# A graph layer with linear attention and experts: rows of x turned beside the products that use them, and attention outputs computed the other way round in two parts

## What is computed

```python
xn = layernorm(x)
# graph part: normalised neighbour sums of h
h = xn @ gnn_W.T + gnn_b
out_g[row] += deg[row]**-0.5 * deg[col]**-0.5 * h[col]      # over all edges and self loops
# linear attention, 16 heads of 64, 256 random features
q, k, v = (xn @ W.T + b for W, b in ...)                      # split into heads
phi(y) = (exp(y @ orf.T / 64**0.25 - |y|**2 / 16) + 1e-6) / 16
kv = phi(k).T @ v ; ksum = phi(k).sum(0)                       # [256, 64], [256] per head
att = (phi(q) @ kv) / (phi(q) @ ksum)                          # per head, rows are nodes
x = x + out_g + att @ Wo.T + bo
# experts: best 2 of 8 by a gate, on layernorm(x)
x = x + ffn(layernorm(x))
```

## Time and profile before

| | |
|---|---|
| median of 3 runs | 1444.85 us (1444.17 to 1446.24) |
| the profiled execution | 1449.3 us, span 1447.7 us |
| TensorE clock granted, mean | 0.97 |
| PE busy | 1359.6 us (94%) |
| DVE busy | 790.5 us (55%) |
| ACT busy | 563.6 us (39%) |
| POOL busy | 395.8 us (27%) |

### The profile page before, as it was taken

One profiled execution on the slowest core, in us unless ns is written; L12 is line 12 of the kernel. 1 busy time (PEld: TensorE's weight loads), 2 busy tenths in 40 slices (PEclk: granted clock), 3 DMA queues, 4 the chain that ended last, 5 costly groups with the idle time before them and its releaser, 6 DMA issues.

```text
span 1447.7 us, 25316 instructions
## 1 busy us (share of the span) xinstructions
PE 1359.6 (94%) x8199; PEld 1201.9 (83%) x8234; DVE 790.5 (55%) x1648; ACT 563.6 (39%) x943; POOL 395.8 (27%) x407
## 2 busy tenths in 40 slices
PE   5899999999989999999999999998999599999996
PEld 2476677899989999999999999987888588888885
DVE  7866444446355656565656565655454634444641
ACT  7322232211044544545454555553222224444541
POOL 7532543244330001010101010003223133333432
PEclk9899999999998999999999999999999599999998
DMA  4111211264410000000000000003245467777853
GB/s 167 49 30 37 66 48 59 77 193 147 119 35 14 30 14 20 24 18 26 16 27 14 29 14 29 0 30 112 57 153 174 172 190 222 219 214 212 275 143 56
DMA packets 58101, 127.78 MB, mean 88 GB/s; under 512 B 7626, under 2 KB 28826, under 8 KB 58048
## 3 DMA queue, kind: packets, MB, share of 16 engines
q1 hardware_dynamic: 48016, 96.79, 20.3%
q0 software_dynamic: 10032, 30.30, 8.6%
HBM read 91.46 MB, written 37.43 MB: 89 GB/s over the span
## 4 chain that ended last, share of the span: by engine, by line
PE 81%; DVE 8%; issue 4%; ACT 3%; DMA 2%; POOL 1%; DVEq 1%; POOLq 0%; SPq 0%; ACTq 0%
PE PB L1757 7%; PE PB L1759 7%; PE PB L1758 7%; PE PB L1663 7%; PE PB L1973 6%; PE PB L1974 6%; PE PB L1976 6%; PE PB L1795 5%; PE PB L1818 4%; PE PB L1742 3%; PE PB L1743 2%; PE PB L1702 2%; PE PB L1744 2%; PE PB L1703 2%; PE PB L1704 2%
## 5 line engine op out<-in xcount | busy, mean ns | idle before, releaser
L1757 PE MATMUL PB<-xh,hw 128*128 128x416 f32 (+1 forms) x576 | 205.6, 357 | 0.0
L1759 PE MATMUL PB<-xh,hw 128*128 128x416 f32 (+1 forms) x576 | 204.5, 355 | 0.0
L1758 PE MATMUL PB<-xl,hw 128*128 128x416 f32 (+1 forms) x576 | 204.4, 355 | 0.0
L1973 PE MATMUL PB<-mwh,mth 128*128 128x512 f32 x368 | 148.5, 404 | 0.6 <-issue 0.6
L1974 PE MATMUL PB<-mwl,mth 128*128 128x512 f32 x368 | 144.2, 392 | 0.0
L724 POOL CAST hw<-hraw 128x1024 fp32r<-128x1024 f32 x24 | 25.0, 1040 | 429.2 <-DVE qphi L1333 207.1
L1663 PE MATMUL PB<-ohs,ohd 128*128 128x512 bf16 (+1 forms) x530 | 114.4, 359 | 16.7 <-DVE ohs L1209 14.4
L1663 PEld LDWEIGHTS PB<-ohs,ohd 128*128 128x128 bf16 x564 | 49.2, 101 | 80.4 <-DVE ohs L1209 43.9
L1209 DVE TENSOR_SCALAR ohs<-iota,sc 128x1280 bf16<-128x1280 f16 x188 | 113.9, 606 | 0.0
L1976 PE MATMUL PB<-mwh,mtl 128*128 128x512 f32 x368 | 113.9, 391 | 0.0
L1757 PEld LDWEIGHTS PB<-xh,hw 128*128 128x128 f32 x576 | 109.9, 191 | 1.4
(11 more groups left out here) (303 smaller groups left out, 3080.4 us busy)
## 6 DMA issues: line engine op xcount, KB each, us to landing
mraw<-expert_w SPq DMA_DIRECT2D x64, 512.0 KB, 9.1
count_rests<-ATf POOLq DMA_DIRECT2D x9, 640.0 KB, 3.5
xrow<-x SPq DMA_DIRECT2D x40, 128.0 KB, 2.9
y_scratch<-xrow SPq DMA_DIRECT2D x40, 128.0 KB, 2.1
yrow<-y_scratch SPq DMA_DIRECT2D x20, 256.0 KB, 3.0
x2n_half<-xhat SPq DMA_DIRECT2D x20, 256.0 KB, 2.3
out<-x SPq DMA_DIRECT2D x9, 512.0 KB
ATf<-wg SPq DMA_DIRECT2D x32, 128.0 KB, 2.3
```

Source lines behind the costliest of these rows:

```text
L1757: mm(bank(i, n), hw[:, wi, 0, k, :], xh[:, k, c0:c0 + n], start=(k == 0), stop=False)
L1758: mm(bank(i, n), hw[:, wi, 0, k, :], xl[:, k, c0:c0 + n], start=False, stop=False)
L1759: ins = mm(bank(i, n), hw[:, wi, 1, k, :], xh[:, k, c0:c0 + n], start=False, stop=(k == KT - 1))
L1973: mm(y[c], mth[:, k, :], mwh[par][:, k, c * CW:(c + 1) * CW], start=(k == 0), stop=False)
```

## The change

Two edits in different stages.

*Head.* (a) Row tile t+1 is turned on TensorE just before product tile t, instead of all ten ahead of the first; tile 0 is turned before block 0. Turned tiles share the PSUM banks of the block that is not being built (TURN_BLOCK). (b) The normalisation of a row tile goes from GpSimd to ScalarE (scale and shift in one pass), for seven tiles at the start and for the last three before block 1. (c) The lows of a quarter of the weights go from GpSimd to VectorE, behind the one-hots of blocks 0, 1, 3 and 6. The raw ring has eight slabs. ScalarE rounds a quarter ahead of a block. (d) `rest_squares(b-1)` comes before the end of block b. (e) The two conversions of the edge lists stand later in VectorE's first chain, and block 0 needs one register load less.

*Attention.* (f) The output product is turned round: stationary is the key-value matrix, moving are the query features over a third of the nodes, and the result has features on partitions, as attnT wants it. The transposes and their copies go. (g) Both operands are split in rounded part and rest: ScalarE adds epsilon and rounds in a second pass after each exponential (qh), VectorE makes the rest (ql) in place of its epsilon pass. (h) The key-value matrix has 128 columns: 64 values and 64 copies of the sum of keys, in one buffer for both heads, so head 1's is made only after outputs(0, 2). (i) VectorE takes reciprocals over 64 partitions x 417 elements and multiplies into attnT. There are three outputs per head, laid between the projections in a new order.

```diff
+TURN_BLOCK = (0, 0, 0, 0, 1, 1, 1, 1, 2, 2)
+EARLY = 7
...
+        def turn_bank(i):
+            return bank(3 * ((TURN_BLOCK[i // 2] + 1) % 2) + i % 3)
...
@@ sync: raw slabs
-                if i >= 4:
-                    sp.wait_ge(w_ready, i - 3)
+                if i >= KT:
+                    sp.wait_ge(w_ready, i - KT + 1)
...
@@ gpsimd
-                g.tensor_scalar(xn_tile(t), xn_tile(t), negmean[:, t:t + 1], rstd[:, t:t + 1], ALU.add,
-                                ALU.mult).then_inc(s_xn, 1)
+                g.tensor_tensor(shift[:, t:t + 1], negmean[:, t:t + 1], rstd[:, t:t + 1], ALU.mult).then_inc(s_shift, 1)
...
+            for t in range(EARLY):
+                row_scale(t)
             degrees(0)
+            for t in range(EARLY, TT):
+                row_scale(t)
+            for b in range(1, TT):
                 degrees(b)
...
@@ scalar
+            def normalize(t):
+                act.wait_ge(s_shift, t + 1)
+                a.activation(xn_tile(t), xn_tile(t), ACT.Identity, bias=shift[:, t:t + 1],
+                             scale=rstd[:, t:t + 1]).then_inc(s_xn, 1)
...
+            normalize_rows(0, EARLY)
             high_quarter(0)
             for i in range(TILES):
                 q, t = i // TT, i % TT
                 if i in BREAKS:
-                    keep_block(BREAKS.index(i) + 1)
-                if i in (11, 22):
-                    high_quarter(2 + i // 22)
+                    b = BREAKS.index(i) + 1
+                    if b in (1, 3, 6):
+                        high_quarter(1 + b // 3)
+                    if b == 1:
+                        normalize_rows(EARLY, TT)
+                    rest_squares(b - 1)
+                if i < TT - 1:
+                    high_turned(i + 1)
+                if i == 0:
+                    keep_block(0)
+                if i in BREAKS:
+                    keep_block(b)
...
@@ scalar, query_exp
+                a.activation(qexp[:, i % 2, c0:c0 + n], bank(3 + f % 2, n), ACT.Exp,
                              scale=PHI_SCALE).then_inc(exp_done, 1)
+                act.wait_ge(exp_done, 2 + 22 * j + f + 1)
+                act.wait_ge(kv_done, START + 2 * j + 2)
+                a.activation(qh[:, i % 2, c0:c0 + n], qexp[:, i % 2, c0:c0 + n], ACT.Identity,
+                             bias=eps[:, :]).then_inc(qh_ready, 1)
...
@@ vector
+            for b in range(TT):
                 one_hots(b)
+                if b == 0:
+                    low_turned(0)
+                if b in (0, 1, 3, 6):
+                    low_quarter((0, 1, None, 2, None, None, 3)[b])
+                for t in range(1, TT):
+                    if TURN_BLOCK[t] == b:
+                        low_turned(t)
...
+            def query_low(j, h, i):
+                v.scalar_tensor_tensor(out=ql[...], in0=qexp[...], scalar=EPS_PHI, in1=qh[...], op0=ALU.add,
+                                       op1=ALU.subtract).then_inc(qph_ready, 1)
...
                 def keep_products(h):
+                    dve.wait_ge(aux_done, START + 10 * j + 7 * h)
                     dve.wait_ge(kv_done, START + 2 * j + h + 1)
+                    v.tensor_copy(kvh[:, :, vals], both_[:, :, 0:DK])
+                    v.tensor_copy(kvh[:, :, dens], sums_).then_inc(kv_high, 1)
+                    v.tensor_tensor(kvl[:, :, vals], both_[:, :, 0:DK], kvh[:, :, vals].bitcast(F32), ALU.subtract)
+                    v.tensor_tensor(kvl[:, :, dens], sums_, kvh[:, :, dens].bitcast(F32), ALU.subtract).then_inc(kv_evac, 1)
...
                 def keep_outputs(h, i):
+                    v.reciprocal(to, bank(6 + f % 2, n)[dens, :]).then_inc(rec_done, 1)
+                    dve.wait_ge(rec_done, 6 * j + 3 * h + i + 1)
+                    v.tensor_tensor(to, bank(6 + f % 2, n)[vals, :], to, ALU.mult).then_inc(aux_evac, 1)
...
@@ vector, pair: new order
+                for i in range(4):
+                    query_low(j, 0, i)
                 keep_outputs(0, 0)
+                for i in range(4, 6):
+                    query_low(j, 0, i)
+                keep_outputs(0, 1)
                     stack_lows(j + 1, 0)
+                keep_outputs(0, 2)
+                keep_products(1)
+                for i in range(2):
+                    query_low(j, 1, i)
                     stack_squares(j + 1, 0)
+                for i in range(2, 4):
+                    query_low(j, 1, i)
                     stack_rests(j + 1, 0)
+                keep_outputs(1, 0)
+                for i in range(4, 6):
+                    query_low(j, 1, i)
                     stack_lows(j + 1, 1)
+                keep_outputs(1, 1)
                     stack_squares(j + 1, 1)
                     stack_rests(j + 1, 1)
+                keep_outputs(1, 2)
                     stack_lows(j + 1, 2)
...
@@ tensor
+            turn_rows(0)
             graph_block(0)
             for i in range(TILES):
                 if i in BREAKS:
+                    if b <= 2:
+                        pe.wait_ge(xt_low, 2 * TURN_BLOCK.index(b))
+                    graph_block(b)
+                if i < TT - 1:
+                    turn_rows(i + 1)
+                if i < TT:
+                    pe.wait_ge(xt_low, 2 * (t + 1))
...
                 def outputs(h, i):
+                    for m in range(MH):
+                        mm(o, kvh[:, m, :], qh[:, m, c0:c0 + n], start=(m == 0), stop=False)
+                        mm(o, kvl[:, m, :], qh[:, m, c0:c0 + n], start=False, stop=False)
+                        ins = mm(o, kvh[:, m, :], ql[:, m, c0:c0 + n], start=False, stop=(m == MH - 1))
...
+                def around_first(k):   # query_features(0, 2) at k = 2, (0, 3) at k = 6
+                def around_second(k):  # query_features(0, 4) at k = 2, (0, 5) at k = 6
+                def around_third(k):   # (1, 0) at k = 0, outputs(0, 2) at 1, (1, 1) at 3, (1, 2) at 5, (1, 3) at 6
...
+                    project_third(j + 1, 0, 0, around_first)
+                    outputs(0, 0)
+                    project_third(j + 1, 0, 1, around_second)
+                    outputs(0, 1)
+                    project_third(j + 1, 0, 2, around_third)
                 outputs(1, 0)
+                for i in range(4, 6):
+                    query_features(1, i)
                 outputs(1, 1)
                     project_third(j + 1, 1, 0)
+                outputs(1, 2)
                     key_features(j + 1, 0, 0)
                     project_third(j + 1, 1, 1)
```

More of the change, by code:

```diff
@@ L77, in gps_layer @@
         dis = keep("dis", [P, TT], F32)
-        sums = keep("sums", [P, TT], F32)
-        negmean = keep("negmean", [P, TT], F32)
-        ssq = keep("ssq", [P, TT], F32)
         varx = keep("varx", [P, TT], F32)
@@ L159, in gps_layer @@
         xn_high = ATf[:, 4:8, :].rearrange("p t n -> p (t n)")[:, 0:TT // 2 * D].rearrange("p (t d) -> p t d", d=D)
-        raw_g = ATf[:, TT - 1, 0:4 * QW].rearrange("p (i n) -> p i n", n=QW)
+        raw_g = [ATf[:, TT - 2 + i // 4, i % 4 * QW:(i % 4 + 1) * QW] for i in range(KT)]
         pb = ExitStack()
@@ L175, in gps_layer @@
         oddi = keep("oddi", [1, TT], I32, pb)
+        sums = keep("sums", [P, TT], F32, pb)
+        negmean = keep("negmean", [P, TT], F32, pb)
+        ssq = keep("ssq", [P, TT], F32, pb)
+        shift = keep("shift", [P, TT], F32, pb)
         pb.close()
@@ L675, in _, with row_scale @@
                 pool.sem_inc(y_copied[c], 2)
-            for t in range(TT):
+            def row_scale(t):
                 pool.wait_ge(ln_a, 3 * t + 3)
@@ L904, in _, with high_turned, normalize_rows @@
                              accum_out=ssq[:, b:b + 1]).then_inc(ln_a, 1)
+            def high_turned(t):
+                for i in (2 * t, 2 * t + 1):
+                    k0 = 4 * (i % 2)
+                    act.wait_ge(xt_done, i + 1)
+                    a.activation(xh[:, k0:k0 + 4, t * P:(t + 1) * P],
+                                 turn_bank(i).rearrange("p (k n) -> p k n", k=4), ACT.Copy).then_inc(xt_high, 1)
+            def normalize_rows(first, last):
+                for t in range(first, last):
+                    row_sums(t)
+                    if t > first:
+                        normalize(t - 1)
+                        if t == 3:
+                            high_turned(0)
+                normalize(last - 1)
             def high_quarter(q):
@@ L1384, in pair @@
                 stack(j, 5)
-                keep_products(1)
-                for i in range(6):
-                    query_eps(j, 0, i)
+                for i in range(4):
+                    query_low(j, 0, i)
                 keep_outputs(0, 0)
+                for i in range(4, 6):
+                    query_low(j, 0, i)
+                keep_outputs(0, 1)
                 if not last:
@@ L1647, in _, with fill_block @@
             mm(PB[0:1, 512 * 7:512 * 7 + 2 * TT], extm[:, :], ident[0:2 * TT, 0:2 * TT], start=True, stop=True).then_inc(s_extr, 1)
+            pe.wait_ge(at_evac, 2)
```

(12 more changed lines are left out.)

238 lines of the change are left out of this document (99 added, 139 removed).

## The result

The changed kernel takes 1505.92 us (median of four runs, 1502.44 to 1509.63) against 1445.53 us (four runs) of the kernel before beside it: a ratio of 1.042, with a 95% interval of 1.039 to 1.045. It is slower by 60 us; 1430.5 was forecast. The profiled execution took 1502.44 us, with a span of 1500.9 us against 1447.7 before.

What follows compares the result with a forecast made beforehand. TensorE, busy 94% of the span, was taken as the bound, VectorE pacing block 0. From the profiled 1449.3 us, -23.8 (head), +7 (seven pairs) and +2.5 (last pair) gave 1435, median 1430.5; range 1412 to 1490.

Steps and rivals of the forecast that it cites:

- The head: All stages before the pairs: -23.8 us in all, between -18 and -28.
- Start and block 0: First count-matrix block: GpSimd no longer slows VectorE's one-hots, -11.0 us; earlier start, -1.5, turn of tile 0 hidden.
- The turning: Head: separate stage of turning x goes, -16.0 us; turns between products, later blocks and ScalarE give back; together -2.4.
- After block 3: Later head, -8.9 us: ScalarE wait gone, GpSimd collisions (-1.7 and -4.5) gone, last degrees 1.0 sooner.
- TensorE's work in a pair: Attention pairs: 36 output products at 0.19 us replace records and turns, -2.8 us per pair if nothing waits.
- The waits: TensorE in a pair: waits sum to 4.3 us, net +1.0 per pair, seven times +7; last pair +2.5.
- Before (1,2): TensorE would wait 3.0 us per pair before query product (1,2), for ScalarE's copies, passes and exponential.
- the three small waits of the forecast: TensorE in a pair: 0.2 us more before (1,3), 0.4 before outputs(1,0), 0.7 before outputs(1,1).
- r: Time of one wide reciprocal on VectorE, 64 x 417: taken as 0.6 us, or 2.3 to 3.0 if by element.
- rival (a): Reciprocal costs by the element, delaying VectorE: +6.6 to +9 us per pair, total 1479 to 1499; chance 0.30.
- one clause in the forecast: Remark that gaps could also lower the granted clock, as in one earlier stretch; no size given.
- the 1.6 us that I gave: Reciprocal time on VectorE from about which its cost decides the sign of the change.

Runs made afterwards that it cites:

- quarters_gpsimd: Kernel before with the change's head alone, but the rests of the weight quarters back on GpSimd: 1430.58 us, ratio 0.986.
- no_division: Changed kernel with each of the 48 wide reciprocals replaced by a copy of the same values, outputs left undivided: 1437.84 us, ratio 0.994.
- half_division: Changed kernel with each wide reciprocal over half the columns only, its result used for both halves: 1488.06 us, ratio 1.031.
- the two added waits: Kernel before with the change's head alone, plus five or two ScalarE copies per pair ahead of query product (1,2)'s work: 1450.82 and 1425.01 us.

## Why the prediction was wrong, step by step

**The head.** Forecast -23.8, measured -29.3 in the traces. Start and block 0: -12.5 forecast; the last one-hot ends at 45.9 instead of 58.3 (the prediction has 58.2), -12.4. The one-hots run at a mean of 542 ns, as forecast. Inside this sum two errors cancel: the first one-hot comes 2.9 us earlier, not 1.5, and the turn of row tile 0 is not hidden but costs VectorE 1.6. The turning: the product after it starts 27.5 us earlier; I priced what comes back until block 3 at 13.6 and found 10.1 (block 3's banks are filled at 114.0 instead of 131.3). A turned tile costs 0.86 us between products, not 1.0, and blocks 1 and 2 lost 1.0 and 1.1 us, not 3.5 together. After block 3 the gain is 12.0 where 8.9 was forecast; quarters_gpsimd says that the collisions with the quarters were dearer than I priced them. The collisions are the ones that the prediction named; the pieces that come back were priced too high and the late collisions too low. What the normalisation alone is worth was overrated: put back on GpSimd it costs 2.0 us in block 0, not 0.8 for each row tile, in good part because the turn of row tile 0 then comes earlier. So the agreement of the first term, -12.5 and -12.4, is partly luck.

**TensorE's work in a pair.** Forecast -2.8, found -2.4 per pair. The output products come every 0.19 us, as taken from the earlier trace rows.

**The waits.** The walk of the queues named the places of the long waits. Before (1,2) 3.0 forecast, 2.71 found, released by ScalarE. Of the three small waits of the forecast, 1.3 us together, no_division shows 0.2 at most, and in six of the seven pairs 0.5 to 0.8 us more than before (0.27) in front of the transposes at L1844, which the walk had not named. With the short operation in the reciprocal's place a pair without clock loss lasts 73.6 us, against 73 to 74 forecast. For r = 2.5 it gave 1.3 and 1.6 us before the key features and 2 to 3 before the key-value products; found at 2.76: 1.39, 1.88 and 2.26. outputs(1,0), put at 2.2, waits 0.2 to 0.9, and outputs(1,1), put at 0.7, 0.1 at most. The last pair, +12 to +15 in rival (a), costs +14.5.

**The step that failed: r.** I took 0.6 us for the wide reciprocal; it takes 2.76. The two short ones had excesses over their neighbours of 29 ns for 5 elements and 42 for 10, 5.8 and 4.2 ns per element, and the line measured is 6.2 per column in all. The evidence was in the rows. Both short rows lie on the measured line: 0.16 us and 6.2 ns per column give 191 and 222 ns, where the rows have 191 and 216. What misled me was the difference of 13 ns between the two excesses, each taken against a neighbour with other operands and another fixed cost; the two reciprocals themselves differ by 25 ns for 5 columns, 5.0 each. The reading by the element and the bounds from it (2.3 to 3.0) were right, and I gave them 0.30.

The Trainium skill, in "VectorE: DVE Perf Modes", walkthrough, fixed hardware budget, calls Reciprocal an iterative divide with a repeat count of 8. The trace agrees with it in kind: the cost is per column, and 4.6 times that of a copy (2.76 against 0.60 us). The estimate of 3.5 us that I worked out from it is too high; at the 0.96 GHz which the same page of the Trainium skill gives, 6.2 ns are an estimated six cycles. The measurement decides.

**What no step had: the clock.** Rival (a) put a pair at +6.6 to +9, waits less the work saved, and the time at 1479 to 1499. Measured, waits and work alone give +4.5 per pair, less than that. On top come 5.7 us per pair of lowered clock, which the prediction had as one clause in the forecast and not as a term, although showed a clock of 0.72 where TensorE was busy half the time. no_division, half_division and the two added waits show it as an effect of waits. Without the clock, rival (a) would have been too high; with it, it is too low. Thus the sign is decided below the 1.6 us that I gave: at r = 1.46 the kernel already takes 1488, and at 0.59 it is 0.6% faster.

**Where the 53 us between the two spans come from.** Head -29.3; seven pairs: work -17.1, waits +48.4, clock +40.1; the last pair +14.5; what remains, -3.5, is the stretch before the first of the seven pairs and the tail.

## What to carry to other kernels

Before an operation is put on many columns, price it per column from whatever short instance the trace has, the excess over its neighbour divided by the elements, and take that as the working value until a row speaks against it. Moving a division from five values per partition to 416 is a change of its cost, not of its place. And when a change opens gaps on TensorE, add the clock to the sum: here waits of 3.4 us cost as much again, and waits of 1.65 us little beyond themselves, though in some pairs the clock also fell after shorter ones (0.8 and 0.6 us in no_division).

## What the runs showed of the hardware

- A reciprocal on VectorE costs 0.16 us and 6.2 ns per column, the same for 1, 64 and 128 partitions and for SBUF and PSUM; a copy of 64 x 418 costs 0.60 us.
- GpSimd's power over 64 x 418 values took 67.05 us, 160 ns per column, and the execution was 69 us longer; it is no way to divide at this width.
- After waits the granted clock fell to 0.50 of full speed. In the pairs it was back at 1.00 after as little as 3 us (behind the 2.71 us in the changed kernel) and as much as 14 (behind the three short waits in half_division); in the pair shown, 0.64, 0.50, then 0.58 from 572 to 576. The same program lost it in some pairs and not in others (0 to 5.6 us in no_division). Which pair loses it, these runs don't say.
- GpSimd's passes over 128 x 256 values slowed VectorE's one-hots of 128 columns from 0.25 to 0.74 us; one pass over 128 x 1,024 slowed a one-hot of 1,280 columns from 0.55 to 1.33.
